# Three late ticks of each plain pass fetched row by row from SyncE

## What is computed

```python
x = layernorm(x + gat(x, edges, edge_attr_64))
x = layernorm(x + cf(x, edge_attr_128, edges))      # messages = xn[dst] * filter, summed by src
x = layernorm(x + gcn(x, edges))                    # sum of normed rows h[src] by dst
x = layernorm(x + gin(x, edges))                    # sum of rows x[src] by dst
```

## Time and profile before

| | us |
|---|---|
| median of three runs (5670.4 to 5691.2) | 5677.1 |
| the profiled execution, time | 5690.5 |
| its span, first to last instruction | 5688.3 |
| GpSimd busy, whole span | 3424.5 |
| VectorE busy, whole span | 2724.1 |
| TensorE matmul busy, whole span | 2596.6 |
| ScalarE busy, whole span | 1096.6 |

### The profile page before, as it was taken

One profiled execution on the slowest core, in us unless ns is written; L12 is line 12 of the kernel. 1 busy time (PEld: TensorE's weight loads), 2 busy tenths in 40 slices (PEclk: granted clock), 3 DMA queues, 4 the chain that ended last, 5 costly groups with the idle time before them and its releaser, 6 DMA issues.

```text
span 5688.3 us, 55800 instructions
## 1 busy us (share of the span) xinstructions
PE 2596.6 (46%) x13812; PEld 2163.6 (38%) x13913; DVE 2724.1 (48%) x8720; ACT 1096.6 (19%) x2627; POOL 3424.5 (60%) x3625
## 2 busy tenths in 40 slices
PE   2677777776566623433343323333333233333333
PEld 2455555655465513323233212322322232333333
DVE  6688777776789723333333323333333333333333
ACT  2676555565410000000000100000000000000000
POOL 2566655665333466666666366666666566666664
PEclk8889888898789855556555555555555555555555
DMA  6555555555289811111111111111111111111111
GB/s 137 123 135 137 125 127 126 130 138 127 49 283 329 259 46 48 50 48 49 49 47 50 30 45 50 49 50 48 50 48 50 38 45 48 49 48 51 48 48 37
DMA packets 458984, 489.95 MB, mean 86 GB/s; under 512 B 87499, under 2 KB 361119, under 8 KB 458662
## 3 DMA queue, kind: packets, MB, share of 16 engines
q0 software_dynamic: 127744, 288.26, 19.4%
q1 hardware_dynamic: 266472, 167.00, 11.1%
q10 hardware_dynamic: 64446, 31.07, 2.0%
HBM read 359.41 MB, written 126.58 MB: 85 GB/s over the span
## 4 chain that ended last, share of the span: by engine, by line
another core or an unknown queue 38%; DVE 20%; PE 13%; issue 13%; ACT 7%; DVEq 5%; DMA 4%; ACTq 1%; POOL 0%; SPq 0%; POOLq 0%
DVE acc L989 10%; PE bank L1762 5%; DMA message_table<-arena 3%; DVEq L764 2%; PE bank L1625 2%; PE bank L1617 2%; ACT arena L1265 2%; DVEq L761 2%; PE bank L1607 2%; DVE arena L1114 1%; ACT arena L1277 1%; DVE arena L1029 1%; ACT arena L1279 1%; ACT arena L1149 1%
## 5 line engine op out<-in xcount | busy, mean ns | idle before, releaser
L1783 POOL DMA_INDIRECT arena<-node_table,pick x1664 | 1613.2, 969 | 871.9 <-issue 480.0
L1762 PE MATMUL bank<-arena 128*128 128x128 f32 x4992 | 1163.2, 407 | 2062.9 <-DVE arena L1029 1562.6
L989 DVE TENSOR_TENSOR acc<-acc,bank 128x128 f32 x2496 | 719.1, 288 | 2471.1 <-remote 1897.9
L1762 PEld LDWEIGHTS bank<-arena 128*128 128x128 f32 x4992 | 1016.8, 302 | 2228.3 <-DVE arena L1029 1668.9
L1783 POOL DMA_INDIRECT arena<-gat_table,pick x832 | 843.2, 1013 | 561.2 <-PE bank L1607 219.9
L1783 POOL DMA_INDIRECT arena<-message_table,pick x832 | 805.3, 968 | 389.0 <-issue 240.5
L1029 DVE TENSOR_TENSOR arena<-iota_free,local 128x512 f32<-128x512 f32 x624 | 430.6, 690 | 0.5
L1617 PE MATMUL bank<-w_L_gnn_We,arena 128*128 128x128 f32 x1568 | 322.4, 330 | 2.2 <-issue 2.2
L1688 PE MATMUL bank<-arena 128*128 x1664 | 258.6, 312 | 119.8 <-DVE arena L1114 90.0
L875 DVE SCALAR_TENSOR_TENSOR acc<-acc,arena,bank 128x129 f32 x832 | 286.8, 345 | 51.8 <-issue 35.0
L1368 ACT ACTIVATE rstd<-moments,eps_col 128x4 f32<-128x4 f32 (+2 forms) x39 | 11.6, 297 | 1512.0 <-DVE moments L1008 772.4
(11 more groups left out here) (266 smaller groups left out, 3207.3 us busy)
## 6 DMA issues: line engine op xcount, KB each, us to landing
message_table<-arena POOLq DMA_DIRECT2D x208, 256.0 KB, 5.3
filter_table<-arena SPq DMA_DIRECT2D x196, 256.0 KB
xt<-edge_cols SPq DMA_DIRECT2D x131, 256.0 KB
arena<-filter_table SPq DMA_DIRECT2D x416, 64.0 KB
arena<-filter_table ACTq DMA_DIRECT2D x416, 64.0 KB
arena<-node_table,pick POOLq DMA_INDIRECT x1664
arena<-edge_cols SPq DMA_DIRECT2D x65, 256.0 KB
arena<-gat_table,pick POOLq DMA_INDIRECT x832
```

The source lines that it names most:

```text
L989: e.tensor_tensor(a, a, bank[6 + t % 2][:, s * P:(s + 1) * P], ALU.add).then_inc(sums, 1)
L1762: ins = e.matmul(bank[6 + n % 2][:, s * P:(s + 1) * P], hot[n % 2][:, s, :], gathered[:, slot(n, s), 0:D], start=True, stop=True)
L1783: e.indirect_dma_start(out=dst, out_offset=None, in_=table, in_offset=bass.IndirectOffsetOnAxis(ap=index, axis=0)).then_inc(done, 16)
```

## The change

TensorE reads the rows of the last three ticks (LATE = 3, 12 steps) of each plain layer not from the ring but from `late`, a buffer of its own on the first part of `xn`. GpSimd gathers the other 205 ticks (GATHERED). The ring's semaphore values follow (`plain_laps`).

SyncE fills `late`. Once, it copies the last 12 columns of both `pick` tensors to HBM (`late_rows`) and reads them back into one partition each (`late_int`). In each layer, `late_in` goes over the 128 partitions: it loads the partition's 12 row numbers into registers, and for each issues a DMA of one row of 512 bytes from the table to one partition of `late`. 28 partitions are done at the start of a layer, and 10 after the table writes of each of the first ten sets; after every such portion SyncE waits until its rows have landed. After partition 127 it raises `late_done`, for which TensorE waits ahead of tick 205. In the second and third layers the first portion waits for the products of the layer before and for all of its table writes.

```diff
+LATE = 3
+GATHERED = TICKS - LATE
+LW = LATE * GRP
+LATE_FIRST, LATE_MORE, LATE_SETS = 28, 10, 10
...
+        late = xn[:, 0:LW, :]
+        late_ints = xn[0:33, LW:2 * LW, :].bitcast(I32).rearrange("p a b -> p (a b)")
+        late_int = [late_ints[32 * k:32 * k + 1, :] for k in range(2)]
...
 (TensorE)
-                    e.wait_ge(ring[n % RT], ring_value(layer, n))
+                    if n < GATHERED:
+                        e.wait_ge(ring[n % RT], ring_value(layer, n))
+                    elif n == GATHERED:
+                        e.wait_ge(late_done, LAYERS[layer])
...
+                        rows_in = (gathered[:, slot(n, s), 0:D] if n < GATHERED
+                                   else late[:, (n - GATHERED) * GRP + s, :])
...
 (GpSimd)
-                for t in range(TICKS):
+                for t in range(GATHERED):
...
 (SyncE)
+            for k in range(2):
+                e.dma_start(late_rows[k * P * LW:(k + 1) * P * LW].rearrange("(p f) -> p f", f=LW),
+                            pick[k][:, STEPS - LW:STEPS]).then_inc(late_kept, 16)
...
+            def late_in(lane, lanes, which, table):
+                for p in range(lane, lane + lanes):
+                    e.load(late_regs, late_int[which][:, p * LW:(p + 1) * LW])
+                    for k in range(LW):
+                        at = e.snap(late_regs[k], min_val=0, max_val=table.shape[0] - 1)
+                        e.dma_start(late[p:p + 1, k, :], table[bass.ds(at, 1), :]).then_inc(late_moved, 16)
+                e.wait_ge(late_moved, 16 * LW * lanes)
+                e.sem_clear(late_moved)
+                if lane + lanes == P:
+                    e.sem_inc(late_done, 1)
+
+            def late_after(n, which, table):
+                if n < LATE_SETS:
+                    late_in(LATE_FIRST + n * LATE_MORE, LATE_MORE, which, table)
...
+            late_in(0, LATE_FIRST, 1, message_table)
             for n in range(NS):
                 e.wait_ge(n2_rows, n + 1)
                 blocks_out(n, 1, tables[0], acc, table_out)
+                late_after(n, 1, message_table)
+            e.wait_ge(plain_product, TICKS)
+            e.wait_ge(table_out, 16 * NB)
+            late_in(0, LATE_FIRST, 0, node_table[0])
             for n in range(NS):
                 e.wait_ge(n3_x, n + 1)
                 blocks_out(n, 0, tables[1], x_sb, table_out)
+                late_after(n, 0, node_table[0])
```

More of the change, by code:

```diff
@@ L60 @@
 AFTER = 18
+LATE = 3
+GATHERED = TICKS - LATE
+LW = LATE * GRP
+LATE_FIRST, LATE_MORE, LATE_SETS = 28, 10, 10
+assert LATE_FIRST + LATE_MORE * LATE_SETS == P
 assert len(PSETS) == NS and PSETS[-1][-1] == NB - 1 and max(READY) == STEPS
@@ L180, in build_program @@
         message_table = dram("message_table", [EW, D])
+        late_rows = dram("late_rows", [2 * P * LW], I32)
         iota_free = sb("iota_free", [P, P])
@@ L370, in build_program @@
         table_out, shifted = sem("table_out"), sem("shifted")
+        late_kept, late_index, late_moved, late_done = (sem("late_" + n) for n in ("kept", "index", "moved", "done"))
         plain_hot, plain_product, plain_summed = sem("plain_hot"), sem("plain_product"), sem("plain_summed")
@@ L379, in build_program @@
         laps = [len(range(k, TICKS, RT)) for k in range(RT)]
+        plain_laps = [len(range(k, GATHERED, RT)) for k in range(RT)]
         def slot(t, s=0):
@@ L386, in ring_value @@
             k = t % RT
-            return 16 * GRP * (LAYERS[layer] * laps[k] + t // RT + 1)
+            before = laps[k] + (LAYERS[layer] - 1) * plain_laps[k] if LAYERS[layer] else 0
+            return 16 * GRP * (before + t // RT + 1)
         def spread_bank(n):
@@ L1761, in plain_layer @@
                     for s in range(GRP):
-                        ins = e.matmul(bank[6 + n % 2][:, s * P:(s + 1) * P], hot[n % 2][:, s, :],
-                                       gathered[:, slot(n, s), 0:D], start=True, stop=True)
+                        rows_in = (gathered[:, slot(n, s), 0:D] if n < GATHERED
+                                   else late[:, (n - GATHERED) * GRP + s, :])
+                        ins = e.matmul(bank[6 + n % 2][:, s * P:(s + 1) * P], hot[n % 2][:, s, :], rows_in,
+                                       start=True, stop=True)
                     ins.then_inc(plain_product, 1)
@@ L2003, in blocks_out @@
                                 src[:, bass.ds(b, 1), 0:D].rearrange("p o d -> p (o d)")).then_inc(done, 16)
+            late_regs = [e.register(f"late_reg{k}").__enter__() for k in range(LW)]
+            def late_in(lane, lanes, which, table):
[11 more added lines that the diff above has]
+                    late_in(LATE_FIRST + n * LATE_MORE, LATE_MORE, which, table)
+            e.wait_ge(m_spread, TICKS)
+            e.wait_ge(late_kept, 32)
+            for k in range(2):
+                e.dma_start(late_int[k], late_rows[k * P * LW:(k + 1) * P * LW].rearrange("(o s) -> o s", o=1)
+                            ).then_inc(late_index, 16)
+            for k in range(MT):
+                e.wait_ge(m_out[k], 16 * len(range(k, TICKS, MT)))
+            e.wait_ge(late_index, 32)
+            late_in(0, LATE_FIRST, 1, message_table)
             for n in range(NS):
@@ L2010, in sync @@
                 blocks_out(n, 0, tables[1], x_sb, table_out)
+                late_after(n, 0, node_table[0])
+            e.wait_ge(plain_product, 2 * TICKS)
+            e.wait_ge(table_out, 2 * 16 * NB)
+            late_in(0, LATE_FIRST, 0, node_table[1])
             for n in range(NS):
@@ L2013, in sync @@
                 blocks_out(n, 0, results, x_sb, out_written)
+                late_after(n, 0, node_table[1])
             e.wait_ge(out_written, 16 * NB)
```

## The result

The changed kernel takes 7388.6 us (median of 4 runs, 7378.2 to 7405.6), the kernel before in the same comparison 5684.1 us (5670.4 to 5706.3): ratio 1.2999, 95% interval 1.2968 to 1.3031. It is slower, as forecast, by 1704 us instead of 1993. The profiled execution took 7388.6 us, its span is 7386.7 us.

What follows compares the result with a forecast made beforehand. GpSimd's gather issue was taken to bound the plain layers. First layer: 1174 us gathers, 711 us remaining rows, 34 us to the next layer; three layers add 1997 us to 5690.5, less 13: 7670 us, range 5640 to 7990.

Steps and rivals of the forecast that it cites:

- (a): GpSimd issues 12 gathers fewer per plain layer: net gain about 20 us in all, at most 53 us.
- (b): SyncE issues 1536 one-row DMAs per layer: 2.54 us each beside gathers, 0.55 us with the gathers over.
- over 2 us: Sign expected in the changed profile: SyncE's rows over 2 us apart before TensorE's standstill, 0.55 us apart in it.
- second rival: SyncE's delay beside gathers grows with DMA size, so a row costs about 1.0 us there: 6470 us; chance 0.28.
- (c): SyncE's 128 loads of 12 registers per layer: 0.063 us per register, about 0.80 us per load, 102 us a layer.
- The time after the gathers: First layer: 1090 late rows left, fetched at the quiet rate with loads, table writes and landings: 711 us.
- (d): Late rows queue on SyncE ahead of table writes; TensorE's tick 205 waits for all; each portion's landing wait about 2 us.
- the step after tick 205: From TensorE's tick 205 to the next layer's first gather: 34 us in the first layer, as before.
- first rival: SyncE isn't slowed beside gathers for such small DMAs, rows come in time: 5657 us, range 5640 to 5677; chance 0.25.
- point of decision: SyncE's cost per row below which all rows arrive before tick 205: 0.65 to 0.70 us.
- third rival: Rows come in time but the DMAs slow GpSimd's gathers by 44 ns each: 5780 us; chance 0.04.

Runs made afterwards that it cites:

- e2: Changed kernel without row fetches (no loads, row DMAs or landing waits; last three ticks' sums not computed) against the kernel before, without stops: 4951.8 against 4976.5 us, ratio 0.9946.
- e12: Changed kernel without row fetches, repeated against the kernel before, again without stops: 4946.1 against 4978.4 us, ratio 0.9936.
- e5: The changed kernel itself, unaltered, measured again against the kernel before, with stops: 7410.7 against 5697.3 us, ratio 1.2994.
- e9: Changed kernel with one late tick in place of three against the kernel before, with stops: 5654.0 against 5643.6 us, ratio 1.0017.
- e7: Changed kernel with row DMAs at fixed addresses (no loads or register operations, wrong rows fetched) against the kernel before, with stops: 5709.8 against 5697.3 us, 1.002.
- e1: Changed kernel with one late tick in place of three against the kernel before, without stops: 4960.4 against 4976.5 us, ratio 0.9967.
- e6: Changed kernel with two late ticks in place of three against the kernel before, with stops: 6402.2 against 5697.3 us, ratio 1.1238.

## Why the prediction was right, and where its terms were off

The mechanism is the one forecast: SyncE, not the DMA engines, sets the pace; the late rows are not in when the gathers end; TensorE's tick 205 waits with every other engine idle. The first layer took 3743.8 - 1958.7 = 1785.1 us instead of the forecast 1919, the second 1838.6 instead of 1898, the third 1804.3 instead of 1907. Of the terms, first layer:

- (a) forecast 20 us net in all, at most 53: 25 and 32 us in e2 and e12, without stops. With the stops it does not show: the gather phase was 1182.7 us (first profile) and 1189.7 (e5), where 1174 were forecast in proportion to 205 ticks, and kernels whose rows are in time take 1.0017 (e9) and 1.002 (e7). That the rows' instructions lengthen the stops would fit; a run with stops and without rows, which would show it, there is none.
- (b) beside gathers: this is the term that was mis-sized. Forecast 2.6 us a row with its share of the load and 446 rows in; measured 1.67 us and 707 rows. The 2.54 us was the mean over 31 sets of table writes, and a row of it stands for 3 instructions just as a late row does. The sets, though, are four DMAs each, close after VectorE's work; SyncE's rows run on through every stretch, 35 and about 70 in 100 us. The forecast said "over 2 us" beside gathers: true of the first 100 us alone. The second rival's 1.0 us was too low and its reason, the size of the transfer, wrong: in the first 100 us a one-row DMA's record is 0.69 us in the median, like that of the register operation, and no shorter than the longest of 128 rows (0.70 to 0.73 us). What counts is the number of instructions: 0.5 to 0.7 us a row at one (e7) against 1.67 at three and a twelfth. In size alone the forecast was no nearer than that rival, whose sum at 1.5 us a row gives 7090 us; 7389 lies midway between it and 7670.
- (b) and (c) with the gathers over: forecast 0.55 + 0.067 us, measured 0.68 us a row, in other shares: row to row 0.43 us on average, less than a 128-row table write, but the load 2.72 us instead of 0.80. The price of 0.063 us per register came from VectorE's load of 16; this load pays 0.2. SyncE's own loads of 16 in the message stage stood in the trace of before (L1983, 52 of them, 0.97 us at the least and 1.72 in the median) and were not used. The Trainium skill has a figure of about 200 ns per register for this instruction ("Runtime: NRT & Kernel Launch", section "Instruction fetch mechanics", on loads of registers from HBM); late_in's loads, from SBUF, agree with it (e1, e6 and e5), the 0.30 us load of four of the earlier trace rows doesn't. The two errors nearly cancel: that the pace with the gathers over came out near the forecast was luck.
- The time after the gathers: 711 us forecast, 566.7 measured. 261 rows fewer at the forecast 0.65 us are 170 us, the dearer row gives some 25 back. In the second and third layers 598 and about 670 rows were in by the gathers' end, and the rest took 644 and 599 us. The three layers end up 134, 60 and 103 us short of their forecasts, which is the gap between 7670 and 7389 but for the place of the medians.
- (d) and the step after tick 205: 35.7 us, forecast 34.
- The first rival (rows in time, 5657 us) is false for this kernel on the chips with stops. On the others SyncE does keep its quiet pace beside gathers: 0.43 us from row to row in e1's stretch, without the load, under the 0.55 us of that rival. Its point of decision, 0.65 to 0.70 us, doesn't carry over, because it counts 0.80 us for a load that takes 2.72 and a gather phase of 1174 us where these chips need some 1040 (e2); whether three late ticks come in time there, no run shows. The Trainium skill's sentence that HWDGE-issued DMAs are immune to that interference ("DMA: Bandwidth & Descriptors", section "SWDGE vs HWDGE vs iDMA") is about VectorE keeping GpSimd from SBUF while GpSimd writes its descriptors. It says nothing of SyncE's instructions beside gathers, so the prediction asked more of it than it states when it let it speak for this rival. In the first profile a register operation is slowed as well: what suffers is SyncE's instruction stream, before any descriptor.
- The third rival (gathers slowed by the DMAs): a gather's mean went from 969 to 964 ns in the last two layers. Out.

What decided the size of the error was one mean over too few and too special places. With the quiet rate in GpSimd's 144 us of stops and 2.6 us elsewhere the sum would have had some 620 rows in instead of 446, as an estimate. That is nearer to the 707, though not how they came: in the stops a row took 1.2 us, and in 570 us beside gathers 1.4.

One reading of the prediction is wrong, without bearing on the sum: that the stops end when GpSimd pauses. VectorE's two stops of the earlier trace rows end at 3278.66 and 3301.06, and GpSimd gathers on through both ends:

```profile
3278.34 0.95 POOL L1783 DMA_INDIRECT arena<-node_table,pick  x1 [0.30 <-issue]
3279.59 0.95 POOL L1783 DMA_INDIRECT arena<-node_table,pick  x1 [0.30 <-issue]
...
3300.10 0.95 POOL L1783 DMA_INDIRECT arena<-node_table,pick  x1 [0.30 <-issue]
3301.36 0.94 POOL L1783 DMA_INDIRECT arena<-node_table,pick  x1 [0.30 <-issue]
```

## What to carry to other kernels

Work moved to an idle queue costs what its instructions cost there, beside what runs then: count every instruction of the inner step (here load, register operation, MOVE, DMA), price each from the same engine in the same state, and compare the total with the time until the data is wanted. Up to that point such a move is nearly free, and beyond it every row costs its full time with the whole core waiting. Where one engine runs far ahead of others that it slows, a shorter lead can be worth more than fewer instructions on it.

## What the runs showed of the hardware that was not expected

- Comparisons on different chips differ: the kernel before takes 5644 to 5697 us in three and 4977 to 4978 in two, 12% apart, and the "remote" waits of ScalarE and GpSimd, and all of VectorE's but 35 us in e12's attention layer, are in the profiles of the former only. GpSimd's gathers have the same pace in both, 1.25 us from start to start. Beside them SyncE's register operation goes from 44 ns to 0.69 us. What holds the engines back the traces don't say. A ratio from one kind of comparison doesn't carry over: one late tick won 0.3% without stops and lost 0.2% with them, the short lead won 1.5% with them and nothing without.
- A DMA of one 512-byte row costs SyncE 0.43 us with its register operation and MOVE, and 0.3 us alone, undisturbed (e7's 23 rows in 6.8 us); the DMA engines were 1% busy with them in the standstill (4 GB/s).
- The load of registers: 0.2 us each in late_in, with row DMAs before it or not; 0.30 to 0.47 us for four in the table writes.
- A load whose registers nobody reads is not in the compiled kernel, so it can't be measured by leaving out its user.
